# Second layers of the expert blocks half in parts, seven places for rows, and a new order for late loads

## The reference, cut to what matters

```
x = x + xattn(ctx, layernorm(x))      # 32 batches of 128 tokens, 256 features, 16 heads of 64
x = x + ffn(layernorm(x))             # 8 experts, 256 -> 1024 -> 256
# ffn, for each of the 4096 tokens:
e    = argmax(x @ centroids.T)        # one expert
h    = relu((xhat * ln_g[e] + ln_b[e]) @ w1[e].T + b1[e])
y    = x + h @ w2[e].T + b2[e]
out  = a * y + (1 - a) * x            # a = sigmoid(x . centroid[e])
```

## Time and profile before

| | |
|---|---|
| median of 3 runs | 1064.18 us (1063.33 to 1064.34) |
| the profiled execution | 1064.58 us, its span 1062.7 us |
| TensorE busy | 1052.9 us, 99% |
| VectorE, ScalarE, GpSimd busy | 797.1, 669.4, 492.0 us |

### The profile page before, as it was taken

How to read it: one execution, slowest core, us unless ns; L and a number is a source line. 1 busy time by engine, 2 the same in 40 slices (tenths; PEclk the granted TensorE clock), 3 DMA queues, 4 the chain that set the end, 5 groups by cost and what they waited for, 6 DMA issues and landing times.

```text
span 1062.7 us, 24108 instructions
## 1 busy us (share of the span) xinstructions
PE 1052.9 (99%) x8466; PEld 943.1 (89%) x8466; DVE 797.1 (75%) x1907; ACT 669.4 (63%) x1820; POOL 492.0 (46%) x647
## 2 busy tenths in 40 slices
PE   9999999999999999999999999999999999999998
PEld 7889898988888888989898888888898999999997
DVE  7878888889888988888898878898886554444441
ACT  6765757576676766575757667676555646566551
POOL 1745464646445554546364645455443442222222
PEclk9999999999999999999999999999999999999999
DMA  6665658585757676765758575666367657766771
GB/s 208 160 170 143 178 144 201 147 211 144 196 142 184 166 193 160 188 171 151 194 145 214 143 199 146 181 155 152 92 169 228 235 198 250 235 227 229 234 245 41
DMA packets 159660, 190.51 MB, mean 179 GB/s; under 512 B 17453, under 2 KB 149037, under 8 KB 154672
## 3 DMA queue, kind: packets, MB, share of 16 engines
q1 hardware_dynamic: 155088, 179.09, 61.6%
q0 software_dynamic: 3360, 8.53, 2.2%
q10 hardware_dynamic: 1088, 1.31, 0.3%
HBM read 65.72 MB, written 46.07 MB: 105 GB/s over the span
## 4 chain that ended last, share of the span: by engine, by line
PE 94%; DVE 2%; DMA 2%; POOL 1%; ACT 1%; SPq 0%; issue 0%; ACTq 0%; POOLq 0%
PE psum L708 16%; PE psum L741 16%; PE psum L883 12%; PE psum L778 11%; PE psum L868 10%; PE psum L757 9%; PE psum L793 9%; PE psum L727 8%; PE psum L796 1%; DVE neg_max L1317 1%; DMA w_ring<-in_w_q 1%; DMA w<-in_experts 0%; DMA prob_t<-w_ring 0%; SPq L573 0%; PE psum L822 0%
## 5 line engine op out<-in xcount | busy, mean ns | idle before, releaser
L1712 POOL TENSOR_TENSOR prob<-prob,inv_sum 128x512 f32<-128x512 f32 x172 | 177.7, 1047 | 194.9 <-DVE inv_sum L1323 194.6
L1317 DVE TENSOR_REDUCE neg_max<-psum 128x2 f32<-128x512 f32 x256 | 162.2, 673 | 33.8 <-PE psum L757 33.7
L1062 ACT ACTIVATE prob<-psum,neg_max 128x256 f32<-128x256 f32 x344 | 160.4, 479 | 37.6 <-DVE neg_max L1317 37.2
L883 PE MATMUL psum<-w,v_n 128*128 128x256 f32 x608 | 134.3, 379 | 0.7 <-DMA w<-in_experts 0.7
L883 PEld LDWEIGHTS psum<-w,v_n 128*128 128x128 f32 x608 | 114.2, 190 | 15.8 <-DMA w<-in_experts 1.0
L1329 DVE STREAM_TRANSPOSE prob<-prob 128x512 f32<-128x512 f32 x172 | 118.7, 699 | 12.3 <-POOL prob L1712 11.9
L1712 POOL TENSOR_TENSOR w_ring<-w_ring,inv_sum 128x512 f32<-128x512 f32 x76 | 78.1, 1041 | 78.6 <-DVE inv_sum L1323 78.3
L1069 ACT ACTIVATE head_out_hi<-psum 128x512 fp32r<-128x512 f32 x52 | 31.1, 598 | 111.4 <-PE psum L778 105.0
L1787 POOL DMA_INDIRECT out<-x_in,r_ring x38 | 39.4, 1036 | 128.9 <-DVE x_in L1561 127.5
L1048 ACT ACTIVATE v_n<-psum 128x512 f32<-128x512 f32 x128 | 78.1, 610 | 26.7 <-PE psum L741 22.7
L1037 ACT ACTIVATE k_hi<-psum 128x512 fp32r<-128x512 f32 x128 | 77.1, 603 | 18.8 <-PE psum L708 18.0
(11 more groups left out here) (189 smaller groups left out, 2716.8 us busy)
## 6 DMA issues: line engine op xcount, KB each, us to landing
sorted_rows<-filler SPq DMA_DIRECT2D x54, 660.0 KB, 5.0
prob_t<-prob SPq DMA_DIRECT2D x172, 128.0 KB, 2.8
w_ring<-prob SPq DMA_DIRECT2D x172, 128.0 KB, 2.7
w<-in_experts SPq DMA_DIRECT2D x19, 1024.0 KB
w_ring<-in_experts SPq DMA_DIRECT2D x18, 1024.0 KB, 5.8
prob_t<-w_ring SPq DMA_DIRECT2D x76, 128.0 KB, 2.8
w_ring<-w_ring SPq DMA_DIRECT2D x76, 128.0 KB, 2.7
w_ring<-normed SPq DMA_DIRECT2D x56, 128.0 KB, 3.0
```

The lines of the kernel that those rows point to most:

```text
L883: last = pe.matmul(bank[:, 0:d_model], hid[:, s % 2, f, i * P:(i + 1) * P], w2[:, f * d_model:(f + 1) * d_model], start=(f == 0), stop=(f ...
L1062: act.activation(prob_at(u, bb)[:, :, parity, i], scores_i, ACT.Exp, bias=neg_max[:, at, i:i + 1], accum_out=prob_sum[:, at, i:i + 1]).the ...
L1317: dve.tensor_reduce(neg_max[:, (4 * u + n) % 8, :], psum[:, n, :].rearrange("p (i j) -> p i j", i=2), AXIS_X, ALU.max, negate=True).then_i ...
L1712: pool.tensor_tensor(probs, probs, inverse, ALU.mult).then_inc(s_soft, 1)
```

## The change

- All blocks but block 0 compute chunks 0 to 3 of the second layer (`FS = FC // 2`) in parts and chunks 4 to 7 plainly (`layer_2_split`). Inside a block the order is parts and plain for the first row half, plain and parts for the second. Block 1 takes plain, parts, parts, plain.
- ScalarE copies the high part of the second weights' first half (`high_weights_2`, 128x1024), GpSimd makes the low part (`low_weights_2`). ScalarE's relu writes chunks 0 to 3 into a single buffer (`hid_raw`) and the others into two (`hid_plain`); VectorE splits the former (`split_hidden`: twice a cast and a subtraction of 128x512). The places are memory that attention has done with.
- Seven places for rows (`NBLOCK`): three more in attention's old query parts; the waits on rows written out move to block s-7, and the vectors wait for the relu of block s-4 only.
- SP's late order: row moves of s, vectors of s+1, rows and first weights of s+2, second weights and `b2` of s.
- VectorE transposes the rows of block s+3 behind `split_xn` of s+2 and ahead of `finish` of s; `finish` adds `b2` straight into the output buffer.
- GpSimd makes base s+2 and low weights s+1, waits for the writes of block s-1, drains, and writes block s; the waits for a block's own writes come in the next block.
- The second weights of block 0 are asked for at the start of step 63, ahead of the moves of step 62's probabilities.

```diff
-NW, NW2, NR = 2, 3, 4
+NW, NW2, NR, NBLOCK = 2, 3, 4, 7
+FIRST_SPLIT = 1
...
@@ sync
                 def load_vectors(s):
-                    if s >= NR:
-                        sp.wait_ge(f_o, 2 * (s - NR) + 2)
-                        sp.wait_ge(f_out[(s - NR) % 2], 32 * ((s - NR) // 2 + 1))
+                    if s == NR:
+                        wait_read(sp, ("h", 3))
+                    elif s > NR:
+                        sp.wait_ge(f_ha, FC // 2 * (s - NR))
...
                 def load_rows(s):
+                    elif s == NR:
+                        wait_made(sp, ("pv", n_steps - 1))
+                    elif s >= NBLOCK:
+                        sp.wait_ge(f_o, 2 * (s - NBLOCK) + 2)
+                        sp.wait_ge(f_out[(s - NBLOCK) % 2], 32 * ((s - NBLOCK) // 2 + 1))
...
+                    if u == n_steps - 1:
+                        wait_made(sp, ("q", n_steps - 1))
+                        load_weights_2(0)
                     if u > 0:
                         move_probabilities(u - 1, 1)
...
                     if u == n_steps - 1:
-                        wait_made(sp, ("q", n_steps - 1))
-                        load_weights_2(0)
                         load_b2(0)
...
-                for s in range(n_early, n_slots + 1):
-                    run(s, (load_vectors,), (load_rows,), (load_weights_1,))
-                    run(s - 1, (load_weights_2,), (load_b2,))
+                run(n_early, (load_rows,), (load_vectors,))
+                run(n_early + 1, (load_rows,))
+                run(n_early, (load_weights_1,))
+                run(n_early + 1, (load_weights_1,))
+                for s in range(n_early, n_slots):
                     run(s, (move_rows,))
+                    run(s + 1, (load_vectors,))
+                    run(s + 2, (load_rows,), (load_weights_1,))
+                    run(s, (load_weights_2,), (load_b2,))
@@ tensor
+                def layer_2_split(s):
+                    pe.wait_ge(f_w2[s % NW2], 16 * (s // NW2 + 1))
+                    pe.wait_ge(f_ha, FC // 2 * s)
+                    def wait_parts(s):
+                        pe.wait_ge(f_w2h, s - FIRST_SPLIT + 1)
+                        pe.wait_ge(f_w2l, s - FIRST_SPLIT + 1)
+                        pe.wait_ge(f_hl, FS // 2 * (s - FIRST_SPLIT + 1))
+                    def in_parts(bank, i, first):
+                        for n, (hw, hx) in enumerate(PASSES):
+                            for f in range(FS):
+                                last = pe.matmul(bank, hid_hl[hx][:, s % 2, f, i * P:(i + 1) * P], w2_hl[s % 2][hw][:, f, :],
+                                                 start=(first and n == 0 and f == 0), stop=(not first and n == 2 and f == FS - 1))
+                        return last
+                    def plain(bank, i, first):
+                        for f in range(FS, FC):
+                            last = pe.matmul(bank, hid_plain[:, s % 2, f - FS, i * P:(i + 1) * P],
+                                             w2_ring[s % NW2][:, f * d_model:(f + 1) * d_model],
+                                             start=(first and f == FS), stop=(not first and f == FC - 1))
+                        return last
...
+                    wait_parts(s)
+                    in_parts(bank, 0, True)
+                    plain(bank, 0, False).then_inc(f_y, 1)
+                    bank = begin(("fy", s, 1))[:, 0:d_model]
+                    plain(bank, 1, True)
+                    in_parts(bank, 1, False).then_inc(f_y, 1)
@@ scalar
+                def relu_parts(s):
+                    b1 = vec_ring[:, s % NR, 2 * KC:]
...
+                    for i in range(FC // 2):
+                        act.wait_ge(f_h, FC // 2 * (s - 1) + i + 1)
+                        if i < FS // 2 and s > FIRST_SPLIT:
+                            act.wait_ge(f_hl, FS // 2 * (s - 1 - FIRST_SPLIT) + i + 1)
+                        elif i == FS // 2 and s >= 2:
+                            wait_made(act, ("fy", s - 2, 1))
+                        for f in (2 * i, 2 * i + 1):
+                            at = slice((f % 2) * BLOCK, (f % 2 + 1) * BLOCK)
+                            dst = hid_raw[:, i, at] if f < FS else hid_plain[:, s % 2, f - FS, :]
+                            ins = act.activation(dst, psum[:, i, at], ACT.Relu, bias=b1[:, f:f + 1])
+                        ins.then_inc(f_ha, 1)
+                def high_weights_2(s):
+                    act.wait_ge(f_w2[s % NW2], 16 * (s // NW2 + 1))
...
+                    act.activation(w2_hl[s % 2][0], w2_ring[s % NW2][:, 0:FS * d_model].rearrange("p (f d) -> p f d", f=FS),
+                                   ACT.Copy).then_inc(f_w2h, 1)
...
                     run(s + 2, (normalise_rows,), (high_weights_1,))
-                    run(s + 1, (relu,))
+                    run(s + 1, (relu_parts,))
                     run(s + 2, (row_gain_bias,))
+                    run(s + 1, (high_weights_2,))
@@ vector
+                def split_hidden(s):
+                    for i in range(FS // 2):
+                        dve.wait_ge(f_ha, FC // 2 * (s - 1) + i + 1)
+                        if i == 0:
+                            wait_made(dve, ("fy", s - 2, 1) if s > FIRST_SPLIT else ("pv", n_steps - 1))
+                        hi, lo = [h[:, s % 2, 2 * i:2 * i + 2, :].rearrange("p f t -> p (f t)") for h in hid_hl]
+                        then_next(dve.tensor_copy(hi, hid_raw[:, i, :]))
+                        dve.tensor_tensor(lo, hid_raw[:, i, :], hi, ALU.subtract).then_inc(f_hl, 1)
...
-                    run(s + 2, (transpose_rows,), (low_weights_1,), (split_xn,))
+                    run(s + 2, (low_weights_1,))
+                    run(s + 1, (split_hidden,))
+                    run(s + 2, (split_xn,))
+                    run(s + 3, (transpose_rows,))
                     run(s, (finish,))
@@ gpsimd
+                def low_weights_2(s):
+                    pool.wait_ge(f_w2h, s - FIRST_SPLIT + 1)
+                    raw = w2_ring[s % NW2][:, 0:FS * d_model].rearrange("p (f d) -> p f d", f=FS)
+                    pool.tensor_tensor(w2_hl[s % 2][1], raw, w2_hl[s % 2][0], ALU.subtract).then_inc(f_w2l, 1)
...
                 row_scales(n_batches - 1)
+                low_weights_2(1)
                 add_base(3)
+                low_weights_2(2)
                 write_rows(1)
...
+                def late_block(s):
+                    run(s + 2, (add_base,))
+                    run(s + 1, (low_weights_2,))
+                    pool.wait_ge(f_out[(s - 1) % 2], 32 * ((s - 1) // 2 + 1))
+                    pool.drain()
+                    write_rows(s)
+                    if s + 1 < n_slots:
+                        with pool.If(empty < n_slots - s - 1) if s + 1 >= n_sure else nullcontext():
+                            late_block(s + 1)
+                    pool.wait_ge(f_out[s % 2], 32 * (s // 2 + 1))
```

151 lines of the change are left out of this document (87 added, 64 removed).

## The result

The changed kernel takes **1052.73 us** in the median of 5 runs (1052.48 to 1054.56), the kernel before 1063.58 (1063.33 to 1064.34): ratio 0.990, 95% interval 0.9886 to 0.9915. By medians 10.85 us are gone, where 9 were forecast, and the time lies 1.3 us under the low end of the range. The kernel before is itself 0.6 us faster here than the 1064.18 that the forecast started from. The profiled execution took 1052.73 us, its span 1050.9, against 1064.58 and 1062.7.

What follows compares the result with a forecast made beforehand. TensorE's queue was taken as the bound: -8.81 (products) + 0.54 (switches) - 0.7 (first block's second weights) = -8.97 us from 1064.58 gave 1055.6, and 0.4 lower for the median, 1055.2 us. Range 1054.0 to 1060.0, about 0.88.

Steps and rivals of the forecast that it cites:

- TensorE's queue laid end to end, changed only in its passes: Expert stage: number and pitch of TensorE's passes set the time; block period from 12.66 to 12.17 us.
- The price of the products: Second layers: a chunk takes 0.3594 us in parts against 0.4206 plain; 0.490 us a block, 18 blocks, -8.81 us.
- The switches: TensorE going from plain f32 to fp32r: three extra at 0.18 us, +0.54 us; nothing if free inside a bank.
- The first block's weights: TensorE's wait for the first block's second weights goes, as their load is issued earlier: -0.7 us.
- The helpers: VectorE, ScalarE and GpSimd busy 8.2, 8.1 and 5.5 of 12.17 us a block, results in time: costed at nothing.
- Seven places, GpSimd's drain, SP's order: Late blocks' row buffers and queue orders: can remove ScalarE's waits, which cost TensorE nothing; 0 us.
- The thin place: Start of the expert stage, blocks 1 and 3: VectorE and GpSimd hold each other up; costed 0, bound 1.5 us.
- rival 1: Early stalls: the thin place breaks or probability moves land late; +0.8 to +3.0 us, 1056 to 1058.2; chance 0.14.
- Rival 2: Late blocks set in part by ScalarE's copy, GpSimd's subtraction and held VectorE: 1058 to 1062 us; chance 0.07.
- Rival 3: VectorE and GpSimd exclude each other fully, their sum of 13.7 us a block being the period: 1080 us; chance 0.05.
- Rival 4: Second layers' parts run at the pace of their loads, 0.19 us, not 0.12: 1085 us; chance 0.03.
- The end: GpSimd's drain at the very end, now waiting for the previous block's writes: 0 us, bound -0.2 to +0.3.

Runs made afterwards that it cites:

- The repeat: The changed kernel run once more, unaltered, as a yardstick on the same chip: 1053.56 us, ratio 0.9894.
- c1: The changed kernel with block 6's first weights asked for ahead of rows and vectors of blocks 6 and 7: 1053.46 us.
- e13: The changed kernel with VectorE's transposes of late rows back at their old place, one block later: 1053.06 us.
- e1: The changed kernel with late second layers alternating chunk by chunk between parts and plain, 7 more switches into parts a block: 1054.38 us.
- e8: The changed kernel with all helpers' work, but all second-layer products plain (chunks 4 to 7 twice, 0 to 3 left out): 1063.9 us.
- e11: The kernel before with second layers half in parts and GpSimd's late loop as changed; four places for rows, SP's and VectorE's old orders: 1067.45 us.
- e5: The kernel before with second layers half in parts and nothing else (the split alone), four places and old orders: 1065.06 us, ratio 1.0018.
- e4: The changed kernel with GpSimd's late loop in the order of before, waiting for each block's own writes: 1061.38 us.
- e10: The changed kernel with SP's late order of before; places and the other engines' orders stay: 1053.9 us.
- e9: The changed kernel with GpSimd's subtraction for the second weights done twice in a row, same outputs: 1068.39 us.
- e3: The changed kernel without GpSimd's nested waits for a block's own writes for blocks 6 to 14: 1053.8 us.
- e14: The changed kernel with four places for rows instead of seven, all its orders kept: 1193.52 us.

## Why the prediction was right, and where it was not

- **TensorE's queue laid end to end, changed only in its passes: right.** The gain is products and one wait, the period 12.09 against 12.17.
- **The price of the products: the step that failed.** It was "0.2103 us a pass" and "going from plain f32 to fp32r costs 0.42 - 0.24 = 0.18 us once". These two are one number cut in the wrong place: 6.73 + 0.18 is 6.91, which is 32 passes at 0.216. I had split the distance between two groups by the start of a record that stands 0.18 us early, and called the remainder a switch. The chain in before had the price without it: 13.83 us for 64 passes, 0.216. With it a block gains 8 x (2 x 0.216 - 3 x 0.120) = 0.58 and 18 blocks 10.4, in place of 8.81 - 0.54 = 8.27. That term alone is 2.1 us, and with it the forecast would have been 1053.1, below the range's low end of 1054.0. The repeat (1053.56), c1 and e13 lie below it as well: the range's low end was too high by this step, not by luck. In the profiled executions the rest is -0.3 for the first weights, +0.8 behind the last write, and -1.25 in attention, which no term had: half of it comes and goes between executions and is luck, the other half (the wait near 660 us) is open.
- **The switches: wrong**, by e1. My lower bound, "nothing, if a switch inside a bank is free", was the case, but the range gave it 0.54 us only: both halves of one reading have to move together.
- **The first block's weights: right in kind, small.** 0.7 was listed; between starts around it about 1.0 is lost, and other executions list up to 1.7. The moves of step 62 do not suffer, as said.
- **The helpers: right for this kernel.** Low weights forecast at T+6.3, ready at T+5.4 (T = 923.61, 929.04); wanted at T+12.2, at T+12.1. Rows forecast at T+15.9 for T+18.6; in the changed kernel at T+15.3 for T+18.4. GpSimd's busy time was underestimated by 2.1 us a block, mostly because its instructions are stretched by VectorE's; that was on no path.
- **Seven places, GpSimd's drain, SP's order: 0 us, "can remove the waits of ScalarE, which cost TensorE nothing".** True where no products change: e8, which has them all and the helpers' new work besides, takes 1063.9 us against 1064.4 beside it (ratio 0.9995, 0.9986 to 1.0005). False as a statement about the change. Without the places the new work costs more than it brings (e11, e5), without GpSimd's order most of it (e4). The step should have asked of each what the new work is worth without it. SP's and VectorE's orders were indeed worth nothing, each taken alone (e10, e13).
- **The thin place.** The mechanism, an instruction held by the other engine of the pair, costs time at block 6, not at blocks 1 and 3: 0 in one profile, 0.8 in the repeat, 1.4 to 1.7 with interleaved products. GpSimd's subtraction for block 1 began at 834.49, 1.6 us sooner than forecast, and its base pair, not VectorE, met the stretch (3.36 us). With that subtraction doubled (e9) the place did break. The repeat's 0.8 is **rival 1** (early stalls) at its lower end, but the time never came near its 1056 to 1058.2.
- **Rival 2 (the helpers' chain)** did not happen, and e4, e5 and e11 show how near it was. **Rival 3 (full exclusion)** is refuted by the changed kernel itself: its own sum, made of unstretched durations, was 8.2 + 5.5 = 13.7 us a block, and the period is 12.09. The busy times as recorded, 8.3 + 7.6 = 15.9, can't refute it, since an instruction's wait for the other engine is counted in them. **Rival 4** is refuted by the 0.120.
- **The end.** "-0.2 to +0.3" for the drain; 0.8 us more behind the last write, of which e3 gives back 0.3. e4, with the loop of before, has 2.5 us there, not the 2.1 it should have had: 0.4 of the 0.8 is open.

## What to carry to other kernels

Take the pitch of a queue from the chain, or from start to same start over a whole period. A remainder between groups of unlike instructions is no price until it is seen to change with their number. And when a change brings new work together with new buffers and orders, ask of each of the latter what the new work would cost without it: buffers that brought nothing without the new work were worth the whole gain with it. The runs of e4, e5, e9, e11 and e14 spread over 5.5 to 7.4 us, those of the other versions over 0.6 to 2.5: here such a spread was itself a sign that a helper's slack had gone.

## What was not expected of the hardware

- **VectorE and GpSimd hold each other out for whole instructions, small ones too.** In the repeat a VectorE subtraction of 128 columns met it:

```profile
855.16 2.73 DVE L1549 TENSOR_TENSOR small<-small,tables 128x128 f32<-128x128 f32 x1
```

The Trainium skill ("SBUF — State Buffer", section "SBUF: two separate sides") calls it a lock for a whole instruction; these rows agree. Yet the two engines' busy times, 15.9 us a block in 12.09, are no bound when added: while one stands, its time is counted as well (2.77 us recorded for 0.69 of work), and VectorE's additions that read PSUM kept their mean of 0.40 to 0.41 us.

- **Writes landed later beside loads.** The indirect DMAs of `out` take 2.4 us from issue to landing at the end of the changed kernel, and 2.2 to 8.1, in the median 4.8, between 860 and 1040 us, among the loads of the late blocks. In e14, where the DMA engines are busy for 0.40 of the time (900 to 1100 us) instead of 0.68, the median is 3.2. A GpSimd queue that waits for its own writes pays this in each block.
- **TensorE's granted clock fell behind some of its waits**: 1.00 (the 2.4 GHz level) in the late blocks of the changed kernel, 0.72 from 955 to 960 us in e4, behind the second of two waits of 2.3 us 14.5 us apart, 0.97 in the mean in the split alone (890 to 990 us) and 0.79 in e14 (900 to 1100), which is between that level and the one of 1.2 GHz. In e11 it stayed at 1.00 over the same 890 to 990, with 6.5 us of shorter waits there (0.2 to 1.7 each).
